# Graph network on Trainium2, first attention stage: query rows as three bfloat16 parts, picked with bfloat16 one-hot matrices

## The reference

```python
q = (embeds[rows] @ qW).reshape(e, HEADS, dh)
k = (embeds[cols] @ kW).reshape(e, HEADS, dh)
v = (embeds[cols] @ vW).reshape(e, HEADS, dh)
scores = jnp.clip(jnp.einsum('ehd,ehd->eh', q, k), -10.0, 10.0)
exp_s = jnp.exp(scores)
norms = jax.ops.segment_sum(exp_s, rows, num_segments=nvar)[rows]
w = exp_s / (norms + 1e-08)
res = jax.ops.segment_sum(w[:, :, None] * v, rows, num_segments=nvar).reshape(nvar, d)
return embeds + res
```

## Time and profile before

| | |
|---|---|
| median of 3 runs | 13133.17 us |
| the profiled execution, span | 13179.5 us |
| TensorE busy | 4527.1 us (34%) |
| weight loads | 3022.1 us (23%) |
| VectorE busy | 6535.8 us (50%) |
| ScalarE busy | 1994.5 us (15%) |
| GpSimd busy | 8151.7 us (62%) |
| mean granted TensorE clock | 0.541 |
| DMA | 1264.02 MB, 96 GB/s |

### The profile page before, as it was taken

The page is one execution under the profiler, slowest core; times in us unless marked ns, Lnnn a source line. Parts: engine busy times, 40 slices in busy tenths (PEclk is TensorE's granted clock), DMA queues, the critical chain, the costliest instruction groups (busy, mean ns, idle before and its releaser), DMA issues. The chain is left out here.

```text
span 13179.5 us, 81573 instructions
## 1 busy us (share of the span) xinstructions
PE 4527.1 (34%) x15877; PEld 3022.1 (23%) x15877; DVE 6535.8 (50%) x10237; ACT 1994.5 (15%) x4360; POOL 8151.7 (62%) x8551
## 2 busy tenths in 40 slices
PE   3354455555222222232222222222222234434443
PEld 3244344444110111111111111111111123333332
DVE  9543344444544454454445455444544544444445
ACT  3233333333100000010000000000000022222223
POOL 1455555555676666656666666766666666666665
PEclk7555555555555555555555555555555555555555
DMA  2355555555333333323333332333333222222222
GB/s 76 106 155 154 149 152 155 153 159 152 99 86 82 87 89 87 88 72 85 87 87 93 81 91 79 87 85 88 89 87 86 81 58 66 69 68 68 68 69 63
DMA packets 1007936, 1264.02 MB, mean 96 GB/s; under 512 B 483123, under 2 KB 740467, under 8 KB 1007331
## 3 DMA queue, kind: packets, MB, share of 16 engines
q0 software_dynamic: 303696, 520.91, 17.5%
q1 hardware_dynamic: 638139, 635.93, 14.8%
q10 hardware_dynamic: 65600, 101.96, 2.7%
HBM read 829.46 MB, written 428.44 MB: 95 GB/s over the span
## 5 line engine op out<-in xcount | busy, mean ns | idle before, releaser
L789 POOL DMA_INDIRECT e_got<-kv_tab,dst_cols x1661 | 1574.5, 948 | 1281.7 <-DVE e_pay L894 770.2
L1843 POOL DMA_INDIRECT e_got<-h_tab,src_tcols x1612 | 1540.9, 956 | 881.8 <-issue 473.8
L1151 POOL DMA_INDIRECT e2a_got<-x_tab,src_cols x1616 | 1531.3, 948 | 775.7 <-issue 556.2
L1151 POOL DMA_INDIRECT e_got<-x_tab,src_cols x1616 | 1553.5, 961 | 718.3 <-issue 586.9
L1151 POOL DMA_INDIRECT e2b_got<-x_tab,src_cols x1616 | 1531.3, 948 | 745.7 <-issue 518.8
L1168 PE MATMUL e2b_EA<-we_W_edge,e2b_attr 128*128 128x384 f32 x808 | 574.9, 866 | 1331.2 <-DVE e2b_emsg L1187 728.3
L1168 PE MATMUL e_EA<-we_We,e_attr 128*128 128x384 f32 x808 | 578.3, 871 | 1297.8 <-issue 898.1
L1168 PE MATMUL e2a_EA<-we_W_edge,e2a_attr 128*128 128x384 f32 x808 | 572.0, 862 | 1300.4 <-issue 767.3
L894 DVE TENSOR_TENSOR e_pay<-e_got,e_Q 128x384 f32<-128x384 f32 x416 | 230.2, 553 | 1570.4 <-ACT e_Q L962 1129.1
L1940 DVE TENSOR_TENSOR_SCAN e_run<-e_Z,e_run,e_msg 98x512 f32<-98x512 f32 x404 | 516.9, 1279 | 795.4 <-ACT e_msg L2005 619.8
L805 PE MATMUL e_Q<-e_window,e_pick 128*128 128x96 f32 x3328 | 758.9, 408 | 79.1 <-issue 41.2
(11 more groups left out here) (373 smaller groups left out, 10316.0 us busy)
## 6 DMA issues: line engine op xcount, KB each, us to landing
scan_out<-e_out SPq DMA_DIRECT2D x416, 200.0 KB
e_window<-q_tab SPq DMA_DIRECT2D x1664, 48.0 KB
scan_out<-e_out SPq DMA_DIRECT2D x404, 196.0 KB
scan_out<-e_out SPq DMA_DIRECT2D x202, 384.0 KB
scan_out<-e2a_out SPq DMA_DIRECT2D x202, 384.0 KB
scan_out<-e2b_out SPq DMA_DIRECT2D x202, 384.0 KB
e_rel<-rel_row ACTq DMA_DIRECT2D x208, 256.0 KB
e_keep<-keep_row ACTq DMA_DIRECT2D x208, 200.0 KB
```

What stands on the lines that cost most here:

```text
L789: e.indirect_dma_start(got[i][:, k, :], None, kv_tab, bass.IndirectOffsetOnAxis(dst_c[:, c * K + k:c * K + k + 1], axis=0)).then_inc(s_g[i ...
L1151: e.indirect_dma_start(got[s % RS][:, k, :], None, x_tab, bass.IndirectOffsetOnAxis(src_cols[:, q:q + 1], axis=0)).then_inc(edge_got[s % R ...
L1843: e.indirect_dma_start(got[c % RG][:, k, :], None, h_tab, bass.IndirectOffsetOnAxis(src_tcols[:, q:q + 1], axis=0)).then_inc(s_g[c % RG], 16)
```

## The change

The queries are kept in `q_tab` as three bfloat16 parts whose sum is the float32 value to its last bits or nearly so: the value rounded to bfloat16, the rest rounded to bfloat16, and the rest of that. A row of `q_tab` has 576 bytes in place of 384. GpSimd makes the parts in the preparation, with four instructions for each of 7 groups; SyncE's store of a group waits for the fourth, ScalarE's next copy into `q_rows` for the second. These instructions stand in GpSimd's order before its gathers. In e0 the windows hold three parts, the picks are bfloat16, and each tile has three products that are added in PSUM in place of one float32 product.

```diff
-    q_tab = scratch("q_tab", (TROW, D))
+    q_tab = scratch("q_tab", (TROW, 3 * D), BF16)
...
+            q_left = ph.sb("q_left", [P, G, D])
+            q_parts = ph.sb("q_parts", [P, G, 3, D], BF16)
...
                     for i in range(NG):
-                        e.wait_ge(a_tab, 3 * i + 1)
-                        e.dma_start(q_tab[i * (G * P):(i + 1) * (G * P), :].rearrange("(g p) d -> p g d", p=P), q_rows[:, :, :]).then_inc(s_q, 16)
+                        e.wait_ge(p_split, 4 * i + 4)
+                        e.dma_start(q_tab[i * (G * P):(i + 1) * (G * P), :].rearrange("(g p) d -> p g d", p=P),
+                                    q_parts[:, :, :, :].rearrange("p g j d -> p g (j d)")).then_inc(s_q, 16)
...
+                    for i in range(NG):
+                        e.wait_ge(a_tab, 3 * i + 1)
+                        if i > 0:
+                            e.wait_ge(s_q, 16 * i)
+                        e.tensor_copy(q_parts[:, :, 0, :], q_rows[:, :, :]).then_inc(p_split, 1)
+                        e.wait_ge(p_split, 4 * i + 1)
+                        e.tensor_tensor(q_left[:, :, :], q_rows[:, :, :], q_parts[:, :, 0, :], ALU.subtract).then_inc(p_split, 1)
+                        e.wait_ge(p_split, 4 * i + 2)
+                        e.tensor_copy(q_parts[:, :, 1, :], q_left[:, :, :]).then_inc(p_split, 1)
+                        e.wait_ge(p_split, 4 * i + 3)
+                        e.tensor_tensor(q_parts[:, :, 2, :], q_left[:, :, :], q_parts[:, :, 1, :], ALU.subtract).then_inc(p_split, 1)
                     for q in range(NT):
...
                             if i > 0 and j == 0:
-                                e.wait_ge(s_q, 16 * i)
+                                e.wait_ge(p_split, 4 * i - 2)
...
-            pick = [ph.sb(f"pick{i}", [P, K, P]) for i in range(4)]
+            pick = [ph.sb(f"pick{i}", [P, K, P], BF16) for i in range(4)]
...
-            window = [ph.sb(f"window{u}", [P, K, D]) for u in range(U)]
+            window = [ph.sb(f"window{u}", [P, K, 3 * D], BF16) for u in range(U)]
...
                         for k in range(K):
-                            ins = e.matmul(Q[c % 3][:, k * D:(k + 1) * D], pick[c % 4][:, k, :], window[c % U][:, k, :], start=True, stop=True)
+                            for j in range(3):
+                                ins = e.matmul(Q[c % 3][:, k * D:(k + 1) * D], pick[c % 4][:, k, :], window[c % U][:, k, j * D:(j + 1) * D],
+                                               start=j == 0, stop=j == 2)
```

More of the change, by code:

```diff
@@ L295, in build @@
             half_col = ph.sb("half_col", [P, 1])
-            zero = ph.sb("zero", [P, HW])
+            zero = ph.sb("zero", [P, 3 * D // 2])
             first_i = ph.sb("first_i", [1, NCH], I32)
@@ L321, in build @@
             p_io, p_set, p_ident, p_node, p_mat, p_tail = (ph.sem("p_" + n) for n in ("io", "set", "ident", "node", "mat", "tail"))
+            p_split = ph.sem("p_split")
             t_tr, t_mm, t_f = ph.sem("t_tr"), ph.sem("t_mm"), ph.sem("t_f")
@@ L370, in _ @@
                     e.wait_ge(p_set, 1)
-                    e.dma_start(q_tab[NROW:TROW, :], zero[:, 0:D]).then_inc(s_z, 16)
+                    e.dma_start(q_tab[NROW:TROW, :], zero[:, :].bitcast(BF16)).then_inc(s_z, 16)
                     e.dma_start(scan_out[EP + 6 * CHS:EP + 6 * CHS + 1, :], zero[0:1, 0:D]).then_inc(s_z, 16)
@@ L374, in _ @@
                         e.dma_start(scan_out[EP + j * CHS:EP + (j + 1) * CHS, :], zero[:, 0:D]).then_inc(s_z, 16)
-                    e.dma_start(scan_out3[EP:EP + 1, :], zero[0:1, :]).then_inc(s_z, 16)
+                    e.dma_start(scan_out3[EP:EP + 1, :], zero[0:1, 0:HW]).then_inc(s_z, 16)
                     e.wait_ge(p_set, 1 + len(we))
```

## The result

After the change the median is 13164.63 us (13142.22 to 13183.57, 15 runs), beside 13145.61 us (13126.07 to 13172.79, 15 runs) for the kernel before on the same chip: ratio 1.0016, 95% interval 1.0009 to 1.0024. So it is slower, by 12 to 32 us. The profiled execution has 13181.2 us of span, 1.7 us more than the one before.

A forecast was written before the change was run, and what follows sets the result against it. SyncE's issue rate was taken to bound e0, and VectorE the preparation. Splits at 25 us, longer rows at 10 and products at 0, added to 13133 us, gave 13168 us, with a range of 13110 to 13290.

The forecast's parts named there:

- e0: The first attention stage, after the preparation, from 438 us to about 3360 us; forecast to begin near 463, about 2930 us long.
- VectorE loses 25 us to GpSimd's splits: Preparation: GpSimd's 28 casts and subtractions hold up VectorE's sort by their data time, 25 us, bounds 11 to 33.
- The two terms: Preparation: data time on 672 elements that VectorE loses, 0.4 us for each of 14 casts, 1.38 for each of 14 subtractions.
- The slots: Preparation: splits fit the groups' 11.8 us; seven row gathers move to about 136 to 148 us, before ScalarE's count needs them.
- Rival 1: Preparation: the splits hide and VectorE loses nothing, giving 13133 to 13143 us; chance 0.15.
- TensorE's gain is worth nothing: Query products in e0: TensorE saves 0 to 0.46 us a chunk, counted as 0 because SyncE's issue covers it.
- Rival 3: e0: shorter products do count, or SyncE stands still less; about 12967 us, or 13110 with a quarter of it; chance 0.14.
- rival 4: Query products in e0: TensorE not shortened at all, 1.87 for 1.86 us, so the forecast time stays; no separate chance.
- Longer rows cost little: Window loads in e0: 576-byte rows make SyncE stand 0.025 us more a chunk, +10 us, ends 0 and 73.
- Rival 2: Window loads in e0: longer rows slow SyncE more than forecast; about 13270 us, up to 13500; chance 0.17.
- SyncE's issue rate is the bound: e0: SyncE's issuing sets the pace, 4.83 us undisturbed plus about 1.9 us standing still, 6.69 us a chunk.
- The sum: Whole kernel: 25 us in the preparation plus 10 us in e0, 35 us on 13133, giving 13168 us (+0.27%).

## Why the prediction was right, and where it was not

The forecast was 13168 us, the measured median 13164.63, and the sign small and slower as said. Some of the closeness is luck: I had put 35 us on a base of 13133.17 us, the median of 3 runs, and over 15 runs the kernel before has 13145.61, from which my sum would have made 13181. The change itself was forecast at 35 us and measured at 12 to 32 on this chip. By its steps:

**VectorE loses 25 us to GpSimd's splits.** Right: e0 begins 24.3, 22.9 and 23.6 us later in three pairs of kernels (the second pair on two chips). The two terms were off in opposite ways: a cast costs 0.54 us for my 0.40, a subtraction 1.14 for 1.38. The slots held as well: the seventh row gather ends at 147.4 us, and ScalarE's count, now at 176.5, doesn't wait for it. Rival 1 is out. The Trainium skill says of this ("SBUF — State Buffer", SBUF: two separate sides) that the pair of ports shared by VectorE and GpSimd is locked for a whole instruction and the loser blocks fully, also where VectorE has two inputs in SBUF and GpSimd's instruction reads SBUF. The trace agrees, with the 2.16 us for 1.02 above. The estimate of 1.46 us, worked out in the prediction from the 2.6 cycles an element of the Trainium skill's "GPSIMD Engine Reference", section 3.1, lies nearer to the 1.3 us between L622's end and the subtraction's than to the 1.14 that VectorE lost.

**TensorE's gain is worth nothing.** Right within some 23 us, and by a larger test than I had priced: the 12 passes take 1.17 us, not 1.40 to 1.87, so the gain was 0.69 us a chunk, 287 us in all, and the two e0 with equal rows differ by 1 us. I had taken the bfloat16 price of another line, which was too dear. Rival 3 is out, and rival 4 too, since TensorE was shortened.

**Longer rows cost little.** Right in kind; 10 us forecast, 21 measured (5 to 36). My reason for the low value, that SyncE's standing doesn't answer to bytes on q1, held only in part: the rows of 1152 bytes show that it does, at a low price. Rival 2's mechanism exists, but not at its price: 36 us where it wanted 67 to 350. It had its price from the search stretch, where gathers are added. The run with half of the gathers shows that these weigh more than DMA time as such: the turn fell to 5.15 us with q1's share at 33.9%, and a DMA share from 1760 to 2600 us of 0.64 for the change's 0.60.

**SyncE's issue rate is the bound.** Half right. SyncE's store is what ScalarE waits for, and SyncE stands because of the gathers; the waits and the run with half of the gathers show this. But I took its rate as a sum, own cost plus standing, in which fewer instructions would save their own cost. That step fell twice: without the store it was slower, and without three of four loads e0 lost 4 to 5 and 9%, not 15 to 27. The standing is not SyncE's own: once SyncE has little to issue and the rows of gathers are long, TensorE stands too.

**The sum** was 35 us. On the first chip the change cost 19 us, on another 42 (24 to 60), and the terms measured singly give 45 or 63. The two measurements of the change overlap only just, at 1.0018 to 1.0024, so whether the chip makes the difference is not settled. One profile of each could not have told the stage's part: in the first pair e0 is 27 us shorter after the change, while the runs on the other chips make the stage some 20 us dearer.

**Open.** Why an instruction often goes through only every 0.7 us or twice that while the gathers run in a row isn't settled. The Trainium skill ("Runtime: NRT & Kernel Launch", Instruction fetch mechanics) has each engine's instructions fetched in blocks of 16 KiB, ahead of use. The trace has such packets (17 in the instruction queue q8 from 1760 to 2600 us before the change, 0.28 MB). I would expect a late block to give one long gap and then full pace, and not single file for ten instructions; no run tests it. That the number of TensorE's instructions counts, and not their time, is not shown. For it speak the one-window kernels: `e_Q` is stretched in 62 of 131 chunks with 12 short passes, in 30 of 138 with 8 long ones and in none of 133 with 4 short ones. Against it, the kernel with 4 is no faster than the one with 8, and these two also differ in row size, form and granted clock (0.50 and 0.61 from 1760 to 2600 us); what holds that kernel is open. It was not tried to pace the gathers by hand, nor to change an engine's instructions with the gathers' rhythm held.

## What to carry to other kernels

Here a saving on an engine that follows a late queue was worth nothing that could be measured, so before making an engine cheaper look who starts last. A cost put on GpSimd was a cost on VectorE, whose instructions had both operands in SBUF: 0.54 us for each cast and 1.14 for each subtraction, near GpSimd's own data time. Where GpSimd's indirect gathers run most of the time, look at the other engines for instructions that come in single file, and measure before giving the gathers more room. The larger prize lay beside the change: one window a chunk with the float32 products is 1.72% faster than the kernel before (12916.11 us) and beats both.

## What the runs showed of the hardware that I had not expected

- TensorE too can go in single file with no semaphore awaited, 0.7 or 1.4 us an instruction, while GpSimd issues gathers in a row. With 14 to 16 in a row it is common in `e_Q` (30 to 62 of some 135 chunks, but none where a chunk has 4 passes), with 5 to 6 it is rare (1 of 128) unless a chunk has 24 (34 of 123).
- Halving the gathers brings SyncE's turn from 6.6 to 5.15 us although q1 carries more, 97 GB/s for 76.
- With a DMA taken out of SyncE's queue (the store) its turn did not get shorter: 7.1 us for four loads, beside 6.9 for four loads and a store.
- A bfloat16 pass of 96 columns in a sequence of 12 costs 0.10 us (1.17 for 12); a float32 one 0.23 (1.86 for 8), both at a granted clock of about 0.5.
